# Selective scan layer: a unit's convolutions are issued two units ahead, its side chain runs earlier, and the output projections run later

## What is computed

```python
xi, z = split(x @ in_w.T)                       # 256 inner features each
u = silu(conv4(xi) + conv_b)                    # 4 taps, per feature
dt, Bm, Cm = split(u @ xproj_w.T)               # 8, 16, 16 columns
delta = softplus(dt @ dt_w.T + dt_b)
dA = exp(delta * A);  dBu = delta * Bm * u      # per token, feature, state (16 states)
h = dA[t] * h + dBu[t];  y[t] = sum_n h_n * C_n[t]      # the scan over 512 tokens
out_d = ((y + u * Dp) * silu(z)) @ out_w.T + x  # for d = forward, backward
out = concat(out_fw, out_bw) @ proj_w.T + proj_b        # then a layer norm
```

## Time and profile before

| what | value |
|---|---|
| median of 3 runs | 4508.89 us (4505.63 to 4517.26) |
| profiled execution, its time | 4514.89 us |
| its span in the trace | 4513.1 us |
| busy over the span: PE, DVE, ACT, POOL | 80%, 59%, 42%, 22% |
| mean granted clock of TensorE | 0.855 |
| first scan to last scan of the layer | 2511.3 to 3652.8 us |

### The profile page before, as it was taken

How to read it: one execution, slowest core, us unless ns; L and a number is a source line. 1 busy time by engine, 2 the same in 40 slices (tenths; PEclk the granted TensorE clock), 3 DMA queues, 4 the chain that set the end, 5 groups by cost and what they waited for, 6 DMA issues and landing times. The chain is left out here.

```text
span 4513.1 us, 50181 instructions
## 1 busy us (share of the span) xinstructions
PE 3613.7 (80%) x13917; PEld 1747.9 (39%) x13917; DVE 2682.5 (59%) x4004; ACT 1892.1 (42%) x3095; POOL 983.9 (22%) x532
## 2 busy tenths in 40 slices
PE   5588886899986598877797677878778777857998
PEld 2122224444443244433443344444444444533443
DVE  6877753433345566535433788888888864265444
ACT  2045562344435044433232565666666632311222
POOL 3100000000002000000000577676767640100000
PEclk7579997899988588878798798888988887878999
DMA  4311110000005322110000333333323220000000
GB/s 132 99 40 55 50 35 26 0 0 0 0 24 161 80 76 75 55 33 0 0 0 20 122 123 113 113 122 113 122 104 123 111 71 3 2 0 0 0 0 19
DMA packets 127683, 250.74 MB, mean 56 GB/s; under 512 B 22245, under 2 KB 97658, under 8 KB 110202
## 3 DMA queue, kind: packets, MB, share of 16 engines
q1 hardware_dynamic: 126506, 247.34, 16.7%
q0 software_dynamic: 1024, 1.58, 0.2%
HBM read 191.98 MB, written 56.89 MB: 55 GB/s over the span
## 5 line engine op out<-in xcount | busy, mean ns | idle before, releaser
L883 DVE TENSOR_REDUCE a_top<-a_sc 128x1 f32<-128x512 f32 (+3 forms) x1024 | 567.3, 588 | 254.5 <-PE a_sc L772 140.9
L1908 DVE TENSOR_TENSOR_SCAN a_g<-a_decay,a_drive 128x512 f32<-128x512 f32 x512 | 607.8, 1207 | 127.1 <-PE a_drive L1608 125.5
L1963 POOL TENSOR_TENSOR a_g<-a_g,a_spread 128x1024 f32<-128x1024 f32 x256 | 615.4, 2410 | 282.6 <-DVE a_g L1908 280.8
L848 ACT ACTIVATE a_prob<-a_st 128x1024 f32<-128x1024 f32 (+2 forms) x512 | 439.5, 865 | 467.3 <-PE a_st L789 294.1
L455 DVE TENSOR_TENSOR f_s<-f_a,f_spread 128x512 f32<-128x512 f32 x392 | 268.1, 687 | 435.4 <-ACT f_a L440 269.0
L769 PE MATMUL a_sc<-a_k,a_q 72*128 72x512 bf16 (+3 forms) x1024 | 399.3, 400 | 138.6 <-DMA a_k<-a_k_rows 63.0
L1802 ACT ACTIVATE a_decay<-a_delta,a_capped_a 128x512 f32<-128x512 f32 x512 | 336.2, 712 | 244.4 <-DVE a_capped_a L1882 178.1
L1586 PE MATMUL a_y<-a_g,ident 128*128 128x512 f32 x768 | 417.1, 671 | 9.2 <-POOL a_g L1963 3.9
L422 PE MATMUL f_y<-f_s,f_w 128*128 128x512 f32 x784 | 401.0, 598 | 20.9 <-DVE f_s L455 20.3
L415 PE MATMUL f_hid<-h,f_w 128*128 x784 | 406.0, 603 | 6.1 <-PEq L246 6.1
L786 PE MATMUL a_st<-a_q,a_k 75*128 75x512 bf16 (+3 forms) x1024 | 307.6, 370 | 18.0 <-ACT a_prob L848 8.0
(11 more groups left out here) (335 smaller groups left out, 5264.7 us busy)
## 6 DMA issues: line engine op xcount, KB each, us to landing
a_spread<-a_bc_rows SPq DMA_DIRECT2D x128, 1024.0 KB, 4.6
a_q<-a_q_rows SPq DMA_DIRECT2D x64, 288.0 KB
a_pv_rows<-a_pv_sb SPq DMA_DIRECT2D x64, 256.0 KB, 2.0
a_q_rows<-p_qp SPq DMA_DIRECT2D x72, 128.0 KB
a_q_rows<-a1q_qp SPq DMA_DIRECT2D x72, 128.0 KB
a_k_rows<-a1q_kp SPq DMA_DIRECT2D x72, 128.0 KB
a_k<-a_k_rows SPq DMA_DIRECT2D x32, 288.0 KB
a_k_rows<-p_kp SPq DMA_DIRECT2D x72, 64.0 KB
```

The lines of the kernel that those rows point to most:

```text
L848: nc.scalar.activation(prob[w % 2][:, j, 0:width(kp)], st[:, j % 2, 0:width(kp)], ACT.Exp, scale=a.scale).then_inc(s.exp_done, 1)
L883: nc.vector.tensor_reduce(top[:, t, n:n + 1], sc[:, t % 2, 0:w], AX.X, ALU.max).then_inc(s.maxed, 1)
L1908: nc.vector.tensor_tensor_scan(g[:, n % 8, k, way], decay[:, n % 4, k, way], drive[:, slot(n, k), way], 0.0, ALU.mult, ALU.add).then_inc(s ...
L1963: nc.gpsimd.tensor_tensor(g[:, n % 8, :, :], g[:, n % 8, :, :], spread[:, pair % 4, 2 + n % 2:3 + n % 2, :].to_broadcast([P, H2, L]), ALU. ...
```

## The change

Six edits, all in the scan layer:

1. **Convolutions.** The two convolutions for unit V = U + 1 leave states 0 and 2 of unit U. Instead, states 12 and 14 of U hold those of W = U + 2. ACT reads them at state 12 and, ahead of `act_begin`, at state 15. Units 0 and 1 get theirs before the first unit.
2. **The rest of the side chain** moves up: z from states 3 and 5 to 0 and 2; xproj from 7 to 4; B and dt from 8 and 9 to 5 and 6; squares from 10 to 12 up to 7, 9 and 10; factors from 11, 11, 12, 13 to 8, 9, 10, 11; delta from 13 to 12.
3. **Output.** `pe_out` moves from state 4 to 8, `pe_project` from 6 to 10, `dve_o` from 5 to 9.
4. `AHEAD` falls from 3 to 2.
5. `pool_du` moves from state 14 to 13.
6. Waits follow: the read of a convolution also waits for the squares and the first factor of the unit between, since they share `soft_t`.

```diff
-    AHEAD = 3
+    AHEAD = 2
...
                 for n in range(STATES):
-                    if n == 0 and not last_unit:
-                        nc.tensor.wait_ge(soft_read, 2 * U + 2)
-                        pe_conv(nb, nd, 1)
...
                     pe_sum_of_slot(U, d, n, first)
...
+                    if n == 0 and not last_unit:
+                        nc.tensor.wait_ge(conv_read, 2 * V + 2)
+                        pe_z(nb, nd, 1)
...
                     if n == 2 and not last_unit:
                         nc.tensor.wait_ge(du_copied, 2 * U + 2)
-                        pe_conv(nb, nd, 0)
...
+                    if n == 4 and not last_unit:
+                        nc.tensor.wait_ge(z_read, 2 * V + 2)
+                        pe_xproj(nd, V)
...
+                    if n == 12:
+                        nc.tensor.wait_ge(soft_read, 2 * V + 2)
                         wait(nc.tensor, o_done, U)
...
+                        pe_conv(b + 1, d, 1)
+                    if n == 14:
+                        nc.tensor.wait_ge(conv_read, 2 * W + 1)
+                        pe_conv(b + 1, d, 0)
...
-                    if n == 5 and not first:
+                    if n == 9 and not first:
                         dve_o(b if d == 1 else b - 1, nd, U - 1)
...
-                    if n == 11:
-                        dve_factor(nd, U + 1, 0)
-                        dve_factor(nd, U + 1, 1)
-                    if n == 12:
-                        dve_factor(nd, U + 1, 2)
-                    if n == 13:
-                        dve_factor(nd, U + 1, 3)
+                    if 8 <= n < 8 + len(LOG1P):
+                        dve_factor(nd, U + 1, n - 8)
+                    if n == 8 + len(LOG1P):
                         dve_delta(nd, U + 1)
...
-                    if n == STATES - 2 and not last_unit:
+                    if n == STATES - 3 and not last_unit:
                         pool_du(1 - d, U + 1)
```

More of the change, by code:

```diff
@@ L1804, in act_decay, with act_unit @@
                 last.then_inc(decay_done, 1)
-            def act_unit(b, d, first, last_unit):
+            def act_unit(b, d, first, last_unit, convs=True):
                 U = 2 * b + d
-                V = U + 1
+                V, W = U + 1, U + 2
                 nd = 1 - d
@@ L2030, in _ @@
                     act_square(0, q)
+                act_conv(1, 1, 1)
+                act_conv(1, 1, 0)
                 act_begin(0, 0)
```

111 lines of the change are left out of this document (54 added, 57 removed).

## The result

The changed kernel takes **4561.86 us**, median of 4 runs (4554.89 to 4565.13), beside 4513.08 us (4505.63 to 4524.62) for the kernel before in the same series: a ratio of **1.0104, 95% interval 1.0077 to 1.0131**. It is slower by 1.0%, about 47 us. The forecast was 4528, with 4484 to 4558 as range: the side is right, the size is not, and the median lies 4 us beyond the upper end.

The account below looks back on a forecast made before the run. DVE's queue was taken as the path, with no engine full. Terms a to e (-5.1 + 1.5 + 0.3 + 2.2 + 2.3) gave +1.2 us a unit, times 15 plus 1 about +19: 4528 us, range 4484 to 4558.

Parts of the forecast that it names:

- e: Handover: DVE's first drives of a unit wait for ACT's copy of du, 2.7 us; +2.3 a unit.
- b: ACT with two decays ahead: scans wait for decays at about state 8; +1.5 us a unit.
- a: DVE's waits for PE's drives, 8.4 us a unit, fall to 3.3, all at state 4; -5.1 a unit.
- d: Four factors and delta on DVE stand against POOL's products: 10.3 us a unit becomes 12.5; +2.2.
- Rival 1: TensorE's clock stays up at state 4 and the handover: -1.5 us a unit, 4487 us, faster; chance 0.15.
- c: Wait before the first factor for ACT's square: 2.0 us becomes 2.3; +0.3 a unit.
- Rival 3: Waits only change places as POOL's phase drifts: -0.6 us a unit, 4501 us, no difference; chance 0.17.
- f: `pe_out`, `pe_project` and `dve_o` at later states: the same instructions, no cost if `bank` is free there.
- g: Once, at the start: two convolutions and their reads before the first `act_begin`; about +1 us.
- rival 2: TensorE's clock is down at state 4 and the handover in every unit: +4.0 us a unit, 4570 us; chance 0.08.
- s: The wait for PE that stays at state 4 in each unit; taken as 3.3 us.
- h: The handover's wait in each unit, DVE's drives for the copy of du; taken as 2.7 us.

Follow-up runs that it names:

- e4: The changed kernel with ACT's decays three states ahead again (AHEAD = 3), nothing else; 4547.05 us, ratio 1.0074 to the kernel before.
- e15: As e14, with PE's second dt product one state later, behind the drives of state 8; 4420.32 us, ratio 0.9784 to the kernel before.
- e14: As e12, with ACT's diagonals at the head of each state's side work; 4412.82 us, ratio 0.9765 to the kernel before.
- e9: The changed kernel with the first convolution, at state 12, computed twice on PE with the same result; 4533.41 us, ratio 1.0054 to the kernel before.
- e3: The changed kernel with factors and delta on DVE directly behind the second scan of their state, ahead of the next drive; 4539.55 us, ratio 1.0053 to before.
- e11: As e7, with factors at states 9 to 12, delta at 13 and `pool_du` at 14; 4387.1 us, ratio 0.9723 to the kernel before.
- e12: As e11, with AHEAD = 3; 4382.8 us, ratio 0.971 to the kernel before.
- e7: The changed kernel with e1 and e3 together, and both PE drives of state 4 ahead of the gate sum; 4447.94 us, ratio 0.9836 to before.
- e6: The changed kernel with factors, delta and `pool_du` back at their old states; 4498.34 us, ratio 0.9951 to the kernel before.
- e1: The changed kernel with ACT's `act_begin` and copy of du ahead of the second convolution's read at state 15; 4505.61 us, ratio 0.9977 to before.
- e2: The changed kernel with PE's second convolution at state 13, between the gate sum and the second drive; 4512.89 us, ratio 0.9992 to before.
- e8: As e7, with AHEAD = 3; 4447.9 us, ratio 0.9853 to the kernel before.
- e10: As e7, with ACT's diagonals ahead of its side reads in each state; 4454.57 us, ratio 0.9864 to the kernel before.

## Why the prediction was half right

The side was right and the mechanism in large part; the sum was short by 2.2 us a unit. Against the forecast's own terms, e was too low by 1.2, b by 0.75 and a by 0.5, and 0.8 fell on an operation that the sum had put at nothing, L1880. d was too high by 0.7, and the small rest is another 0.5 below (rounded; a and b by units 4 to 13). So no single term explains the whole; e is the largest.

**a, right in kind.** State 10's wait went, state 4's grew to 3.8 (3.3 was taken, 1.3 to 4.2 the ends), because the gate sum ran at the lower clock. Two of PE's stretches on each side of it (after):

```profile
3118.00:3123.00 5.00, 1.16 (x8) 0.97 (x8) 5.00 (x6) 4.16 (x5) 3.94 (x2) 0.97 0.40 170
3123.00:3130.00 7.00, 5.20 (x13) 3.15 (x14) 3.37 (x4) 4.84 (x8) 4.80 (x3) 0.53 0.24 98
```

In the first PE worked 1.16 of 5 us; in the second the granted clock was 0.53, near the lower level of 1.2 GHz, and the sum took 3.75. Where the clock stayed up, in e4, the same sum took 1.96 and the wait was 1.3. Rival 1, which wanted 1.3 here and 2.0 at the handover, is refuted in both places.

**b, right in place, wrong in cause.** 1.5 was taken at state 8, as a wait of scans for decays, for want of a third pair. 2.25 was measured and the releaser is PE's drive. e4 puts the third pair back and state 8 does not gain. PE's drive stands behind the second dt product (3139.53 and 3140.58 in its timeline above), a stand that part a had declared past; e15 beside e14 shows that this is worth 2.7 of 5.0 there. What is not settled is how much each of ACT's reads, the bank and the rest of PE's order adds: in unit 8 the last drive and the decay end within some tenths of each other.

**c, right:** 2.2 for 2.3.

**d, right by the rule, with one operation missed.** First factor 1.84 (2.3 was said), then 3.02, 3.02, 1.19 and delta 3.01, place for place as worked out. The unit's mean for the five is 11.9, where 12.5 was said and 10.3 stood before. The rule that whoever begins second stands until the first is done had been applied to the five large operations and to no other. L1880 begins at 3172.50, in the middle of this product in POOL's timeline (after):

```profile
3167.78 2.35 POOL L1960 TENSOR_TENSOR a_g<-a_g,a_spread 128x1024 f32<-128x1024 f32 x1 [0.71 <-DVE a_g L1909]
3170.20 3.21 POOL L1965 TENSOR_TENSOR a_g<-a_g 128x1024 f32<-128x1024 f32 x1
```

The product ends at 3173.41 and L1880 at 3173.44. That is the 0.8 a unit of this operation. Delta stood behind the first of the two in the same way. The reduction just before it, beside the same product, took its usual 1.22: not every DVE operation stands. The Trainium skill, "SBUF — State Buffer", section "SBUF: two separate sides", names those with two SBUF inputs and those "in a 2-port perf mode" as the ones that want the pair; `tensor_scalar` is on its list of those that can enter such a mode, and `tensor_reduce` on this chip never contends. The trace agrees with both: 0.94 in place of 0.17, and 1.22 as ever. By that list of the Trainium skill L1880 was a candidate, and the sum left it out. Rival 3, a drifting phase, did not come: the pattern is the same in unit after unit.

**e is the step that failed.** It had the right chain and a wrong size, 2.7 where 3.9 was measured (58.8 over 15): "I take 2.7, a quarter of the way", between 2.0 at full clock and 4.6 at the half level. In unit 8 DVE's own part from the first scan of state 13 took 8.0 (7.9 was said), and the chain 11.7 in place of 9.9. Of these 1.8 the drive is 1.0 and the convolution 0.5; with the next unit's slower one (5.3) the wait is 4.9, so 4.3 in the mean of units 4 to 13. The upper end, 4.6, had put the convolution alone at the half level and left the drive ahead of it at 0.9.

The quarter was chosen because convolutions now fill the end of a unit. But delta and what follows on DVE keep PE without work for some 3.8 us, in every unit, just ahead of the chain; the granted clock is 0.66 over the 5 us behind 3098, and the drive takes 2.08 in place of 1.05 in every unit but the first. e9 fills that time, and the wait is 2.3. The stretch to ask about was the one right in front of the chain, not the mean over four states; and it could be estimated from the trace of the kernel before, where delta and the small operations behind it take DVE from 3079.91 to 3085.24, beside a convolution on PE that the change takes away from there.

**f** cost what it was said to, nothing that shows. **g**, put at +1, does not show either: from PE's first projection to dt, B and C to the first scan it is 30.5 before and 29.6 after.

Of the rivals, **rival 2** was the nearest, the clock down at both places: s = 3.8 and h = 4.3 where it had 4.2 and 4.6. It had 0.08 on the ground that states 12 to 15 gain 7 us of PE work; they do, but one convolution ends ahead of delta and the other is in the chain itself. With its s + h - 4.8 the measured pair gives 3.3 a unit, and 3.4 is what the layer shows. That this agrees so well is luck in part: the terms that the formula took as given were off as well, b by +0.75 and d by -0.7, L1880 is not in it, and h is 3.9 over the whole layer.

## What to carry over

When a side chain moves ahead, ask of every engine's queue what now stands in front of the handover: here one read ahead of one copy cost 56 us, more than the whole move lost, and one sum ahead of one drive 46. Where a chain starts on TensorE just after it was left without work, look up what the first operations took in such a place, and cost them at the lower clock if they did. And place DVE's two-input operations directly behind what POOL waits for, if POOL has time to spare, but then cost the small ones that follow too. Alone (e3) that kept less than a third of its gain: 30 of 73 went to an operation on two numbers and 27 to the next two waits; beside the two swaps, and with its inputs given one state more (e11, e12), the kernel came out 3% faster than before.

## What the runs showed of the hardware beyond that

- **A two-number operation can cost more than a large one.** TENSOR_SCALAR on 128x2 takes 0.17 by itself, 0.94 (L1880) in the changed kernel, and 2.18 (the second one) in e3 and e7, where a factor on 128x1024 takes 1.20. Each time it ended within 0.03 us of POOL's product.
- **More work, less time.** With a redundant convolution of some 3.4 us a unit, e9 is 23 to 28 us faster than the changed kernel; in the stretch that holds it and the chain behind it the granted clock is 1.00, where the changed kernel has 0.66 at the chain's start.
- **The loop's round.** DVE's gap at it is 1.3 at most before, and 2.7 to 3.0 in e1 with no engine named. Five rounds together cost 5.6 before and 5.1 to 5.6 in e6, e11, e12, e14 and e15, but 13.9 to 14.6 in e1, e2, e7, e8 and e10. Why they are long in the kernels with delta at state 12 and a copy of du in time, and short with delta at state 13, was not tried and stays open.
